# A fused Mamba block and ternary FFN on one core: the first half of a chunk's head is issued 4 to 20 half steps sooner, and the small steps at the chunk boundary stand in another order

## What is computed

```python
def mamba(x, ...):                       # d_inner 512, N = 16 states, 4 conv taps
    h = x * rsqrt(mean(x*x) + EPS) * norm_w
    u, z = split(h @ in_proj_w.T)
    uc = silu(conv_b + sum(up[:, k:k+L] * conv_w[:, k] for k in range(4)))
    dt, B, C = split(uc @ x_proj_w.T)
    dt = softplus(dt @ dt_proj_w.T + dt_proj_b)
    # for every token: state = exp(dt * A) * state + dt * B * uc;  y = sum_n state * C
    y = (scan(dt, A, B, C, uc) + uc * D) * silu(z)
    return y @ out_proj_w.T + x
def ffn(x, ...):                         # 256 -> 1024 -> 1024 -> 1024 -> 256, ternary weights
    h = silu(x @ w1 * s1) * (x @ w2 * s2)
    return gelu(gelu(h @ h1 * t1) @ h2 * t2) @ w3 * s3
x = x + layernorm(mamba(layernorm(x)))
x = x + layernorm(ffn(layernorm(x)))
```

## Time and profile before

| what | us |
|---|---|
| median of 3 runs | 1887.0 (1885.42 to 1889.71) |
| the profiled execution's own time | 1884.17 |
| its span, first to last instruction | 1882.4 |
| busy: PE, DVE, ACT, POOL | 1439.8, 1328.0, 1240.7, 1182.0 |
| mean granted TensorE clock | 0.864 of full |

### The profile page before, as it was taken

The page is one execution under the profiler, slowest core; times in us unless marked ns, Lnnn a source line. Parts: engine busy times, 40 slices in busy tenths (PEclk is TensorE's granted clock), DMA queues, the critical chain, the costliest instruction groups (busy, mean ns, idle before and its releaser), DMA issues.

```text
span 1882.4 us, 30131 instructions
## 1 busy us (share of the span) xinstructions
PE 1439.8 (76%) x9080; PEld 1258.1 (67%) x9080; DVE 1328.0 (71%) x1962; ACT 1240.7 (66%) x2622; POOL 1182.0 (63%) x1503
## 2 busy tenths in 40 slices
PE   4566677777787887878778887777788887786975
PEld 2122567776786876777777776677777776775865
DVE  2677887777778686777778786778778786777410
ACT  4354575868578675868668675868668675857443
POOL 1543757676667667676667767676667767767322
PEclk8687798889798988899898988899798988897887
DMA  3222100101001010101001010101001010101000
GB/s 101 102 89 73 39 21 19 41 25 36 25 19 42 19 42 20 41 23 37 24 20 42 19 42 20 40 24 36 22 24 42 19 42 19 35 24 30 3 8 7
DMA packets 38934, 63.76 MB, mean 34 GB/s; under 512 B 5216, under 2 KB 19424, under 8 KB 38640
## 3 DMA queue, kind: packets, MB, share of 16 engines
q10 hardware_dynamic: 18944, 33.83, 6.0%
q1 hardware_dynamic: 19696, 26.02, 4.3%
HBM read 55.38 MB, written 4.46 MB: 32 GB/s over the span
## 4 chain that ended last, share of the span: by engine, by line
PE 26%; POOL 22%; issue 19%; ACT 16%; DVE 15%; POOLq 1%; ACTq 1%; DVEq 0%; DMA 0%; SPq 0%
POOL S L469 12%; PE fP L615 6%; DVE S L1130 6%; PE fP L616 6%; PE sT L639 4%; ACT dA L870 3%; PE hP L603 3%; PE fP L603 3%; DVE acc L1144 3%; ACT Rw L1039 2%; POOL Glo L540 2%; PE fP L736 2%; PE fP L737 2%; ACT L1039 1%; POOL x L571 1%
## 5 line engine op out<-in xcount | busy, mean ns | idle before, releaser
L469 POOL TENSOR_TENSOR S<-X,Bs 128x1024 f32<-128x1024 f32 x256 | 609.7, 2382 | 371.7 <-PE sT L639 277.2
L1130 DVE TENSOR_TENSOR_SCAN S<-dA,S 128x512 f32<-128x512 f32 x512 | 621.6, 1214 | 174.2 <-ACT dA L870 97.7
L870 ACT ACTIVATE dA<-delta,A 128x255 f32<-128x255 f32 x1024 | 446.5, 469 | 382.6 <-DVE S L1130 243.9
L615 PE MATMUL fP<-Ghi,w_h 128*128 128x256 f32 x2048 | 548.0, 304 | 58.9 <-ACT Rw L1033 27.7
L616 PE MATMUL fP<-Glo,w_h 128*128 128x256 f32 x2048 | 524.8, 293 | 0.0
L615 PEld LDWEIGHTS fP<-Ghi,w_h 128*128 128x128 f32 x2048 | 414.0, 202 | 70.8 <-ACT Rw L1033 34.5
L1144 DVE SCALAR_TENSOR_TENSOR acc<-sT,CT,acc 128x512 f32<-128x512 f32 x480 | 351.5, 735 | 108.3 <-PE sT L639 106.2
L639 PE MATMUL sT<-ident,S 128*128 128x128 f32 x2048 | 345.0, 300 | 103.7 <-DVE acc L1144 89.7
L616 PEld LDWEIGHTS fP<-Glo,w_h 128*128 128x128 f32 x2048 | 414.3, 202 | 0.4
L639 PEld LDWEIGHTS sT<-ident,S 128*128 128x128 f32 x2048 | 262.8, 154 | 169.9 <-DVE acc L1144 95.2
L540 POOL TENSOR_TENSOR Glo<-Rw,Ghi 128x1024 fp32r<-128x1024 f32 x96 | 225.8, 2355 | 120.1 <-ACT Ghi L1045 105.6
(11 more groups left out here) (136 smaller groups left out, 1981.2 us busy)
## 6 DMA issues: line engine op xcount, KB each, us to landing
Bs<-b_rows ACTq DMA_DIRECT2D x128, 256.0 KB, 3.1
Rw<-in_h SPq DMA_DIRECT2D x11, 512.0 KB, 3.3
xh<-in_x SPq DMA_DIRECT2D x16, 256.0 KB, 2.9
xt<-in_x SPq DMA_DIRECT2D x16, 256.0 KB, 3.0
out<-x SPq DMA_DIRECT2D x16, 256.0 KB, 2.2
x<-in_h SPq DMA_DIRECT2D x5, 512.0 KB, 3.2
Rw<-in_w SPq DMA_DIRECT2D x4, 512.0 KB, 4.6
w_in<-in_in_proj SPq DMA_DIRECT2D x1, 1024.0 KB, 5.2
```

Source lines behind the costliest of these rows:

```text
L469: pool.tensor_tensor(s[:, :, :], X[par][:, :, :], row[:, None, :].broadcast_to([P, DT, T]), ALU.mult).then_inc(scan_pool.sem, 1)
L615: pe.matmul(dst, w[:, i, cols_], hi[:, i, :], start=(j == 0), stop=False)
L870: a = act.activation(dA[half][:, i, 1:], delta[par][:, d, 1:], ACT.Exp, scale=A[:, d * N + n:d * N + n + 1])
L1130: a = dve.tensor_tensor_scan(pair, dA[half][:, :, :].rearrange("p d t -> p (d t)"), pair, 0.0, ALU.mult, ALU.add)
```

## The change

- The scales of both norms move from POOL's hs 3 and 4 of body c to hs 17 of body c-1 (`ahead_step`), behind the product of n=10; the statistics on DVE from hs 3 to hs 16 of the body before, `hn` on ACT from hs 6 to hs 28 of the body before. SP loads the row at the start of a body.
- PE transposes hn at hs 0 (was 8), `hT` is made by DVE at hs 1 (was ACT, 9). In_proj: quarters 0 and 1 at hs 2 behind yT, 2 at hs 5, 3 at hs 6 (was 10 to 13). ACT copies z at hs 4, u at 6 and 7, and makes cbase at 7 (was 11 to 14). The halo copy moves from DVE hs 10 to ACT hs 4. DVE's taps stand at 11 to 13 (was 15 to 17).
- x_proj and all behind it stay.
- ACT's gelu block moves from hs 31 to hs 0 of the next body, behind `front`, and the rounding of half 1 from hs 0 to hs 1.
- POOL's tail steps of hs 5 and 7 (o scales, x1) stand ahead of `front`. `carry_in` moves from hs 30 to 29, and the exp of `first_decay` on ACT to hs 29.

```diff
@@ gpsimd
+            def ahead_step(h):
+                pool.wait_ge(ahead_vec.sem, ahead_vec.at(h, "x_aggr"))
+                normal(ahead_ln, h, "", hmv, hsm, 0)
...
             def head_step(h, hp, hs, first):
-                if hs == 3:
-                    pool.wait_ge(head_vec.sem, head_vec.at(h, "x_aggr"))
-                    normal(head_ln, h, "", hmv, hsm, 0)
                 if hs == 4:
...
-                if hs == 30:
+                if hs == 29:
                     carry_in(h, 0, first)
...
+                    if tail and hs in (5, 7):
+                        tail_step(c - 1, 1 - par, hs)
                     if scan and hs % 2 == 1 and n + 2 < N:
                         front(c, par, n + 2)
                     if end and hs not in (1, 13):
                         end_step(c - 2, par, hs)
-                    if tail:
+                    if tail and hs not in (5, 7):
                         tail_step(c - 1, 1 - par, hs)
                     if head:
                         head_step(c + 1, 1 - par, hs, prepare if head_seq_start is None else head_seq_start)
+                    if head and another(c) and hs == 17:
+                        ahead_step(c + 2)
@@ tensor
-                if hs == 8:
-                    pe.wait_ge(head_act.sem, head_act.at(h, "hn"))
+                if hs == 0:
+                    pe.wait_ge(ahead_act.sem, ahead_act.at(h, "hn"))
...
-                if 10 <= hs < 14:
-                    q = hs - 10
+                for q in {2: (0, 1), 5: (2,), 6: (3,)}.get(hs, ()):
@@ scalar
+            def halo(h, first):
+                ahead, last = u_ext[:, :, 0:CONV - 1], u_ext[:, :, T:T + CONV - 1]
...
+                    act.copy(ahead, last).then_inc(head_act.sem, 1)
...
+            def ahead_step(h):
+                act.wait_ge(ahead_ln.sem, ahead_ln.at(h, "nmr12"))
+                act.wait_ge(head_pe.sem, head_pe.at(h - 1, "hT"))
+                normed(hn, xh, hsm, 10).then_inc(ahead_act.sem, 1)
+            def head_step(h, hp, hs, first):
+                if hs == 4:
+                    halo(h, first)
+                    act.wait_ge(tail_pe.sem, tail_pe.at(h - 2, "out"))
+                    for q in range(2):
+                        act.wait_ge(head_pe.sem, head_pe.at(h, f"z{q}"))
+                        act.copy(z[hp][:, 2 * q:2 * q + 2, :], hP[(q + 1) % 2][:, :, :]).then_inc(head_act.sem, 1)
+                if hs in (6, 7):
+                    q = hs - 6
                     act.wait_ge(head_pe.sem, head_pe.at(h, f"u{q}"))
                     act.copy(u_ext[:, 2 * q:2 * q + 2, CONV - 1:], hP[(q + 1) % 2][:, :, :]).then_inc(head_act.sem, 1)
-                if hs == 14:
+                if hs == 7:
...
             def end_step(g, gp, hs):
                 if hs == 0:
+                    m = HM - 1
+                    gelu(g, tail_act, f"h1_{HM // 2 - 1}", 0)
+                    scaled(g, tail_act, tail_pe, f"h1_{m}", m, ring(1 - gp, f"h1_{m}"), c_("h1_s", m))
+                    round_half(g, tail_act, "gelu1_0", 0)
+                    gelu(g, tail_act, f"h1_{m}", 1)
+                    act.preload_act_table_set(LN_EXP)
+                if hs == 1:
                     round_half(g, tail_act, "gelu1_1", 1)
...
+                    if head and another(c) and hs == 28:
+                        ahead_step(c + 2)
@@ vector
+                if hs == 1:
+                    dve.wait_ge(head_pe.sem, head_pe.at(h, "hT"))
+                    for k in range(KM):
+                        a = dve.tensor_scalar(hT[:, k, :], hP[0][:, k, :], c_("norm_w", k), None, ALU.mult)
+                    a.then_inc(head_vec.sem, 1)
+                if hs in (11, 12, 13):
+                    k = hs - 11
...
+                    if head and another(c) and hs == 16:
+                        ahead_step(c + 2)
```

More of the change, by code:

```diff
@@ L184, in build @@
                         ["stats", "aggr"])
+        ahead_act = Steps(sem("ahead_act"), ["hn"])
         head_act = Steps(sem("head_act"),
-                         ["hn", "hT", "z0", "z1", "u0", "u1", "cbase", "silu0", "silu1",
+                         ["halo", "z0", "z1", "u0", "u1", "cbase", "silu0", "silu1",
                           "zs", "dtx", "ct", "v0", "v1", "e", "l", "first_decay"])
@@ L262, in build, with another @@
         HALVES = 2 * N
+        def another(c):
+            return not (isinstance(c, int) and c + 2 >= CHUNKS)
         def stages_at(c, hs):
@@ L359, in body @@
                      seq_start=None, head_seq_start=None, j=None):
+                if head and another(c) and not (isinstance(c, int) and c == 0):
+                    load_row(c + 2)
                 if isinstance(c, int) and c == 1:
@@ L839, in _ @@
         def _(act):
-            start(act, head_act, decay_act, carry_act, tail_act, end_act, b_stored, b_in[0], b_in[1])
+            start(act, ahead_act, head_act, decay_act, carry_act, tail_act, end_act, b_stored, b_in[0], b_in[1])
             for landed in b_in:
@@ L904, in normed, with clear, shift @@
                 return a
[L906 to L924, removed]
+            def halo(h, first):
+                ahead, last = u_ext[:, :, 0:CONV - 1], u_ext[:, :, T:T + CONV - 1]
+                def clear():
+                    act.wait_ge(carry_clear, 2)
+                    act.wait_ge(head_vec.sem, head_vec.at(h - 1, "tap2"))
+                    act.copy(ahead, zeros[:, :, None].broadcast_to([P, DT, CONV - 1])).then_inc(head_act.sem, 1)
+                def shift():
+                    act.wait_ge(head_vec.sem, head_vec.at(h - 1, "tap2"))
+                    act.copy(ahead, last).then_inc(head_act.sem, 1)
+                if isinstance(first, bool):
+                    if first:
+                        clear()
+                    else:
+                        shift()
+                else:
+                    with act.If(first):
+                        clear()
+                    with act.Else():
+                        shift()
@@ L962, in head_step @@
                     load_B(h, hp, (hs - 24) // 4)
+                if hs == 29:
+                    act.wait_ge(head_pool.sem, head_pool.at(h, "first_rate"))
+                    act.activation(first_decay[:, :, :], first_decay[:, :, :], ACT.Exp).then_inc(head_act.sem, 1)
                 if hs == 26:
@@ L1094, in body @@
                         round_stage(s)
+            ahead_step(0)
             iterate(act, body)
@@ L1099, in _ @@
         def _(dve):
-            start(dve, head_vec, scan_vec, acc_vec, tail_vec, end_vec)
+            start(dve, ahead_vec, head_vec, scan_vec, acc_vec, tail_vec, end_vec)
             for half in range(2):
```

80 lines of the change are left out of this document (32 added, 48 removed).

## The result

The changed kernel takes **1974.67 us** (median of 4 runs, 1971.1 to 1983.64) against 1888.36 for the kernel before on the same chip: ratio 1.0464 [1.0424, 1.0503]. Slower, as forecast, but by 86 us and not by 45; it lies above the range of 1856 to 1966. The profiled execution has a span of 1973.1 us and a mean granted clock of 0.834.

A forecast was written before the change was run, and what follows sets the result against it. No engine is full; waits between engines in fixed order bound the kernel. Bodies 2 to 13 add 6 x 3.4 + 6 x 4.3 = +46; with the other bodies +45 on 1884.2, so 1929, median 1932 us, range 1856 to 1966.

The forecast's parts named there:

- The sign: Whole kernel: slower was given 0.69, the same 0.05, faster 0.26.
- The gelu block behind `load_B`: Body boundary: ACT's block behind `load_B` makes product 2 later by 4.2 us (body 8) and 5.4 (body 9).
- The scales behind product 10: POOL, half step 17: 6.1 us of scales make product 11 later by 4.2 us (body 9: 5.1).
- x1's gain: POOL: scales gone from half steps 3 and 4 and the new order bring x1 0.7 us sooner (body 9: 1.6).
- the second gelu block: ACT: early quarters, u copies and cbase make this block start 2.4 us later, at 965.3 instead of 962.91.
- D: Head: x_proj stays at half step 20, so nothing of the next scan starts sooner; part of the forecast, no separate chance.
- w3: PE: no longer behind 3.53 + 1.73 us of in_proj; its second half ends 2.1 us after the low part, at 977.6.
- product 9: POOL: follows product 8 at 978.1 instead of 979.99, 1.9 us sooner (body 9: 1.0).
- Rival C: PE idles some 6 us before w3, whose 4.0 us become 7 at low clock: +36, 1968 us; chance 0.13.
- Rival A: Faster: the scales are covered if product 10 comes more than 5.3 us sooner: 35 us less, 1852 us; chance 0.25.
- the waits that it counts as removed: For the faster case: 2.2 us of halo, 4 of DVE behind x1, 3.5 of in_proj quarters.
- the order of o's scales and x1: POOL: o scales and x1 ahead of the products; x1 no longer waits for a 2.6 us product, repaying the boundary.

The follow-up runs named there:

- e6: The kernel before with only ACT's first gelu block moved behind `load_B` to half step 0, its last rounding at half step 1: 1944.15 us, 1.031.
- e2: The changed kernel with both norms' scales on POOL ahead of product 10 (half step 16), their statistics on DVE at 14: 1911.31 us, 1.0122.
- e3: The changed kernel with both edits, gelu block back at half step 31 and norm scales ahead of product 10: 1844.76 us, 0.9763.
- e5: The changed kernel with 5 extra throwaway matmuls on PE ahead of w3: 1955.96 us, 1.0369.
- e11: e3 with 5 extra throwaway matmuls on PE ahead of w3: 1830.28 us, 0.9717.
- e13: e12 with 5 extra throwaway matmuls on PE ahead of w3: 1781.97 us, 0.9443.
- e8: The kernel before with only the halo copy moved from DVE to ACT, same half step 10: 1878.31 us, 0.9965.
- e7: e3 with hn transposes, `hT`, in_proj quarters, z and u copies, halo, cbase and taps at old half steps (`hT` on DVE, halo on ACT): 1833.04 us, 0.9724.
- e10: e7 with POOL's o scales and x1 behind the products of half steps 5 and 7 again: 1897.11 us, 1.0068.
- e14: The changed kernel with POOL's o scales and x1 behind the products of half steps 5 and 7 again: 2002.78 us, 1.0616.
- e1: The changed kernel with ACT's gelu block back at half step 31 and the rounding of half 1 at half step 0: 1915.84 us, 1.0150.
- e9: e7 with both norms' scales on POOL behind product 10 again (half step 17, statistics at 16): 1881.35 us, 0.998.
- e12: e3 with z's quarters and copies early, but u's quarters at 12 and 13, their copies, cbase and taps late: 1801.97 us, 0.9566.

## Why the prediction was right, and where it was not

**The sign, and the two costs, were right.** The gelu block behind `load_B`: forecast +4.2 / +5.4 at product 2, measured +4.7 / +5.6, shown alone by e6 (+4.7 / +5.9). The scales behind product 10: forecast 6.1 us on POOL, measured +5.8 from product 10 to 11 in even and odd bodies, shown by e2. x1's gain (-0.7 / -1.6, measured -0.9 / -1.5) and the second gelu block (+2.4, measured +2.5) came out to 0.2 us. D, that the head's gain starts nothing of the next scan sooner, fits: the kernel with the early in_proj (e3) is not faster than that with the late one (e7). The Trainium skill, VectorE: DVE Perf Modes, "Mode 2×_2P", was weighed with no row for `hT` on DVE; now there is one, never near the 2.2 us of the halo copy, though 17 of the 32 lie wholly inside a product of POOL:

```profile
L1200 DVE TENSOR_SCALAR e_sp<-hP,col x32: 460/476/484, 13.7 to 1648.0; 128x256 f32<-128x256 f32 x32
```

So the trace agrees with that page for an operand in PSUM.

**The step that failed is w3**: "Its second half needs the low part (975.5), then 2.1 us: it ends at 977.6", and with it product 9 at -1.9 / -1.0. The low part is where the forecast had it: its end in the body is +2.0 / +1.4, forecast +1.9 / +1.7. What follows it took 5.3 / 4.4 us and not 2.1. Over six even and six odd bodies that is 6 x 3.2 + 6 x 2.3 = 33 us. Two things are in it. The count: behind the second low part stand 24 of w3's 32 matmuls, not 16, 3.1 us at full clock, so 1.0 us a body or 12 in all. And the clock: 2.2 / 1.3 us a body on top, 21 in all.

Product 9 is +3.0 / +1.1, which is 4.9 / 2.1 us later than forecast, 42 us in twelve bodies. Some 7 of the 9 us that w3 leaves are the base: I walked through body 8, whose product 9 stands at 62.1 us into the body, where the even bodies' mean is 61.0. Body 8 is the one body of the twelve in the kernel before in which quarter 2 took 3.53 us behind a wait of 4.0; in ten of them it takes 1.99 at 1.00 behind a wait of 1.8 to 2.6. So the forecast credited w3 with a slow quarter that it mostly does not stand behind. Of the 42 us, 37 reach the length of the bodies (+82.6 against +46). The profiled execution is 46 us above the forecast's 1929; the other 9 are body 14 (5.5), what lies ahead of body 2 (6.1) and what lies behind body 14 (-2.4), and no run took those apart.

**Rival C was this mechanism, and I gave it 0.13.** Its condition was that w3 is last at that place, "which it is by 2 us". I counted it as a case outside the forecast because a w3 that begins early seemed able to hide its low clock. But only its first 8 matmuls begin early. The rest waits for the low part with a pause in front of it, and everything behind that pause is paid. e5, e11 and e13 show the clock's price by adding work to PE and nothing else: 19, 14 and 20 us come back. That C's 1968 lies so near 1975 is in part luck: it has 36 us for the clock, where 21 were measured, and neither the count nor body 14. The Trainium skill, TensorE: Matmul & The Clock Gate, "Part 1: The HAM clock gate", holds the low clock for the default that activity lifts; the trace agrees, with 0.50 behind idle stretches and 1.00 behind the five extra matmuls.

**Rival A** is near in its number, and not by its terms. With both placements put right (e3) the rest of the change is worth 42 us, beside A's 35. But of the waits that it counts as removed, the halo copy alone is worth 8 us (e8), and the quarters moved away from w3, as the change places them, gain nothing (e3 against e7). And the scales, which A needed covered, are not covered behind product 10.

**Sized too low**: the order of o's scales and x1. I costed it as 2.6 us of x1 that repay the boundary. Taken out, it costs 64 us in e7 (e10) and 28 in the changed kernel (e14); nearly half of the 64 is the clock of quarters 2 and 3, for which the forecast has no term. This is not what the order is worth in the kernel before: there the old order leaves quarter 2 at 1.00 in ten of twelve bodies, and no run gave that kernel the new order alone. The 53 us by which e7 beats the kernel before are not taken apart either: of its parts only the halo (e8) was run alone, and `hT` on DVE, `carry_in`, `first_decay` and the norm scales moved ahead were not.

**Misread in the rows**: the earlier trace rows give DVE 24.1 us idle in body 8, not "26 us or more"; no term of the sum rests on it.

The runs form a chain from e7 (1833) to the changed kernel: early in_proj +12 (e3), scales behind product 10 +71 (e1), gelu block at half step 0 +59, together 1975. The steps add up by construction, and their size depends on the kernel that they are made in: the scales cost 48 us in e9 and 63 by e2.

**What was to be seen**: product 2 done 19 to 20 us behind the first scan: yes, 964.17 to 984.1. ACT's pause ahead of `load_B` some 10 us: 8.4. PE longer for xdbl: 6.4 instead of 1.4. Product 11 about 4 to 5 us later in the body: 9.0 and 6.9. Bodies of 109 to 112: 112.4 and 113.6, the w3 step again in both.

## What to carry to other kernels

A block of an in-order engine that lies just in front of a long wait can be free; just behind the wait it is paid, here with 4 to 5 us a body of its 5.9 (e6). The same holds for the 20 tiny operations of the norm scales: before you move them, look at which product they stand behind and where the engine pauses. And when you move matmuls away, ask for the granted clock of those that stay: they may have kept PE at its full clock for a product that others wait for. A few throwaway matmuls in the pause can then pay (five did, in three kernels), too many do not (twelve cost 21 us). And read such a place in more than one body: body 8 was not like the others.

## What the runs showed of the hardware

- In the changed kernel PE idles 1.0, 2.7 and 1.9 us ahead of and inside w3 (body 8), and w3 runs at 0.50, the 1.2 GHz level. In ten of twelve bodies its last 24 matmuls of 128x256 took 4.5 to 5.5 us instead of 3.1. In e12 w3's first 8 matmuls ran at 1.00 and a pause of 2.9 us followed in each of bodies 2 to 13; the 24 behind it ran at 0.50 to 0.66. In e13 the pause was 1.6 us and they ran at 1.00.
- Quarter 2 of in_proj, eight matmuls behind a wait of PE: in the kernel before, e6, e7, e8, e9 and e10 it ran at 0.50 to 0.61 behind 3.8 to 4.0 us, in all 16 bodies that have such a wait; behind 1.8 to 2.6 us it ran at 1.00 in 48 of 56 bodies and at 0.66 to 0.79 in the other eight.
- The halo copy, 160 to 2314 ns on DVE, takes 185 to 207 ns on ACT, and moving it alone is worth 8 us by the medians (e8).
